# Query and key stacks sent group by group through a ring of five, the experts' bias as one product over 24 rows, and a moved first half-stack, in a three-layer decoder kernel

## The chip, the cores and the metric

The kernel runs on one core of one Trainium2 chip. The metric is the device time in microseconds (us) of one execution, lower being better. A second, profiled execution gives the trace that is read here.

## The reference, cut to what matters

The input is x, 8 batches of 512 tokens by 256 features, and a context of the same shape. Three layers follow each other, each ending in x = layernorm(x + layer(x)):

```
layer 1: q,k,v = x@Wq+bq, x@Wk+bk, x@Wv+bv (128 wide); state = 0.99*state + 0.01*v k^T
         out_t = state_{t-1} q_t ; y = out@Wo + bo
layer 2: 16 heads of 16, q from x, k and v from ctx: softmax(q k^T / 4) v, then @w_o + b_o
layer 3: attn = softmax(q k^T / 4) v with 16 heads, q,k,v from x@W_qkv+b
         gate = softmax(x@W_gate+b); combine = the two largest gates of 8, others 0
         moe = sum_e combine_e * (x@W_e + b_e)          (b_e: the experts' bias, 8x256)
         layer = attn + moe
```

## The kernel before, in words

There are two attentions for each of the 8 batches, so 16 phases in the order C0, C1, S0, C2, S1, ..., S7 (C is the cross attention of layer 2, S the self attention of layer 3). A phase has 4 groups of 4 heads, and a group takes 4 slots, one for each block of 128 keys. A slot has two halves; "slot 82.1" below is the second half of slot 82. In each half TensorE (PE in the profile) computes in this order: two score products into the PSUM tile `sc` (`scores`, two heads, once ScalarE has taken the exponentials of the half before), two products into `mx` for the row maxima of the group that is 6 slots ahead (`max_tiles`), and in the first half of a slot the eight products of probabilities and values into `op` (`values`). VectorE (DVE) reduces each `mx` tile to a maximum; ScalarE (ACT) takes the exponential of `sc`. `max_tiles` waits until the tile two back has been reduced, as there are three `mx` banks.

Everything else is cut into units (a projection, four transposes, an expert product `moe0` to `moe15`, ...), and tables such as `LIN`, `MID_LONG` (batches 1 to 6), `MID_SHORT` (batches 0 and 7) and `MOE_LONG` place each in a slot and half relative to the phase of its batch. `plan_units` makes one list out of it, sorted by half and, within a half, by the loops' order (shift, moe, middle units, first-layer units, heads). TensorE runs the units of both halves of a slot in the second half, after `sc` and `mx`. Units use two PSUM banks of the tile `ms` in turn, so a unit waits until the unit two places ahead of it in the list has been taken out (`unit`: `wait_unit_out(pe, *ORDER[u - 2])`). For the split units (`kc`, `qc`, `k3c`, `q3c`, which make the rows of the half-stacks) taken out means that ScalarE wrote the high part (`high`, L698) and after it VectorE the low part (`low`, L838). For `be0`, `be1` it means ScalarE's copy into `moe`.

The two parts of q and k are then stacked on partitions: 16 high rows, 16 rows of the other part and 16 again for each of the two sides, 48 rows in all, in the tiles `qs` and `ks`. This is done by transfers within SBUF, issued by the SP queue in program order (`stack`, L399): six for a half-stack of two groups, 128 KB each, into a ring of three half-stacks. The row maxima of a group go through a transposition (`shift` unit, L552), a copy to `shift_r` (L892) and two more SP transfers (`shift`, L410) into `qs`; the first score of a group waits for them. In the table a group g has its `shift` unit in slot 4g-2 and its first score in slot 4g.

The gate's choice of experts runs on VectorE in `choose` and `choose_end` (L1011 to L1042), whose last result is `comb`. The unit `combT` transposes `comb` (L594), and `be0`, `be1` multiply it with the 8x256 bias in plain fp32, which the profile shows as two passes for each product (four instructions in a unit).

Of the kernel before, what the change touches and what calls it, by code (L numbers as in the profile page):

```python
# [25 lines left out]
PAIRS = H // SIDES  # L26
HALF = PAIRS // DC
RING = 3
# [22 lines left out]
LIN_SECOND = {"q1": (-13, 1), "k1": (-6, 1), "v1": (-14, 0), "s0": (-5, 1), "s1": (-4, 1), "s23": (-3, 1),  # L51
# [182 lines left out]
STAGED = ("we", "wqkv3")  # L234
# [8 lines left out]
def decoder(nc, x, xT, ctxT, w, out):  # L243
    with ExitStack() as ctx:
# [21 lines left out]
        combT = o1T[0:E, :]  # L266
# [6 lines left out]
        qs = sb("qs", [P, RING, HALF, T])  # L273
        ks = sb("ks", [P, RING, HALF, T])
# [21 lines left out]
        above = sb("above", [P, TB, E, E])  # L296
        tied = sb("tied", [P, TB, E, E])
        rank = sb("rank", [P, TB, E])
        comb = sb("comb", [P, TB, E])
        moe = sb("moe", [P, 2, 512])  # L300
        we_part = (sb("we_hi", [P, DC, E * D]), sb("we_lo", [P, DC, E * D]))
# [12 lines left out]
        w_first, w_in, w_late, we_in = sem("w_first"), sem("w_in"), sem("w_late"), sem("we_in")  # L314
        scaled, we_cut, w3_in, w3_cut, fills = sem("scaled"), sem("we_cut"), sem("w3_in"), sem("w3_cut"), sem("fills")
        x_in, xT_in, ctx_in, y_out = sem("x_in"), sem("xT_in"), sem("ctx_in"), sem("y_out")
        stack_in = {"k": sem("stack_k_in"), "q": sem("stack_q_in")}
# [16 lines left out]
        G_STEPS = 12  # L334
# [30 lines left out]
        def stack_of(g):  # L365

            return 2 * (g // G) + g % G // 2

        @block.sync
        def _(sp):  # L370
# [16 lines left out]
            def stack(name, e):  # L387

                dst, which = (ks, K_PART) if name == "k" else (qs, Q_PART)
                sp.wait_ge(part_low[name], e + 1)  # L390
                if e == 0:
                    sp.wait_ge(fills, 5)
                if e >= RING:
                    sp.wait_ge(score, 2 * 8 * (e - RING + 1))
                    sp.wait_ge(max_t, 32 * (e - RING + 1))
                for side in range(SIDES if (name, e) != ("q", 0) else 1):
                    for r in range(TERMS):
                        at = 64 * side + HD * r
                        sp.dma_start(dst[at:at + HD, e % RING, :, :],  # L399
                                     part[name][64 * side:64 * side + 64, which[r], :]).then_inc(stack_in[name], 16)  # L400

            def shift(g):

                sp.wait_ge(shift_out, g + 1)
                wide = HG // SIDES
                first = wide * (g % 2)
                for side in range(SIDES):
                    at = 64 * side + ROWS
                    rows = SHIFT * wide * TB
                    sp.dma_start(qs[at:at + SHIFT, stack_of(g) % RING, first:first + wide, :]  # L410
                                 .rearrange("a h (n t) -> a (h n) t", n=TB),
                                 shift_r[rows * side:rows * side + rows, g % 2, :]).then_inc(shift_in[g % 2], 16)
# [21 lines left out]
            for c in range(DC):  # L434
                sp.dma_start(we_stage[c], w["we"][:, c, :]).then_inc(we_in, 16)
            for t in range(FIRST_HALF, LAST_HALF + 1):
# [12 lines left out]
        def _(pe):  # L449
# [55 lines left out]
            def unit(task, n):  # L505
# [85 lines left out]
                elif task == "combT":  # L591
                    pe.wait_ge(g_step, G_STEPS * (n + 1))
                    for t in range(TB):
                        last = nc.tensor.transpose(bank[0:E, t * P:t * P + P], comb[:, t, :], ident[:])  # L594
                elif task in ("be0", "be1"):
                    wait_unit_out(pe, "combT", n)
                    for j in range(2):
                        t = 2 * int(task[2]) + j
                        last = mm(bank[:, j * D:j * D + D], combT[:, t * P:t * P + P], W["be"][:], True, True)
# [13 lines left out]
            def max_tiles(i):  # L613

                g, pair, t, _ = head_tile(i)
                e = stack_of(g)
                if i % 32 == 0:
                    for name in "kq":
                        pe.wait_ge(stack_in[name], 16 * TERMS * SIDES * (e + 1))
                if i >= 2:  # L620
                    pe.wait_ge(max_out, i - 1)
                for side in range(SIDES):
                    at = 64 * side
                    mm(mx[:, (i + side) % 3, :], qs[at:at + ROWS, e % RING, 2 * (g % 2) + pair, t * P:t * P + P].bitcast(F32R),
                       ks[at:at + ROWS, e % RING, 2 * (g % 2) + pair, :].bitcast(F32R), True, True).then_inc(max_t, 1)

            def scores(s, h):

                g, kb = s // TB, s % TB
                e = stack_of(g)  # L630
# [4 lines left out]
                for side in range(SIDES):  # L635
                    at = 64 * side
                    last = mm(sc[:, side, :],
                              ks[at:at + ROWS + SHIFT, e % RING, 2 * (g % 2) + h, kb * P:kb * P + P].bitcast(F32R),
                              qs[at:at + ROWS + SHIFT, e % RING, 2 * (g % 2) + h, :].bitcast(F32R), True, True)
# [54 lines left out]
        def _(act):  # L694
# [5 lines left out]
            def high(task, n):  # L700
# [4 lines left out]
                if e >= 1:  # L705
                    act.wait_ge(stack_in[name], 16 * TERMS * SIDES * e)
# [3 lines left out]
            def take_out(task, n):  # L710
# [23 lines left out]
                elif task == "combT":  # L734
                    wait_unit(act, task, n)
                    copy(combT, bank[0:E, :]).then_inc(done, 1)
# [6 lines left out]
                elif task.startswith("moe"):  # L743
# [3 lines left out]
                    act.wait_ge(g_step, G_STEPS * (n + 1))  # L747
# [41 lines left out]
            for t in range(FIRST_HALF, LAST_HALF + 1):  # L789
# [28 lines left out]
                if t == lin_at("qc0", 0) + 1:  # L818
                    act.wait_ge(part_low["q"], 1)
                    for i in range(TERMS):  # L820
                        act.dma_start(qs[64 + HD * i:64 + HD * i + HD, 0, :, :],
                                      part["q"][64:128, Q_PART[i], :]).then_inc(stack_in["q"], 16)
# [8 lines left out]
        def _(dve):  # L831
# [172 lines left out]
            def choose(n):  # L1004
# [17 lines left out]
                nc.vector.tensor_tensor(above[:], theirs, mine, ALU.is_gt).then_inc(g_step, 1)  # L1022
                nc.vector.tensor_tensor(tied[:], theirs, mine, ALU.is_equal).then_inc(g_step, 1)

            def choose_end(n):

                def g_wait(k):
# [4 lines left out]
                nc.vector.tensor_tensor(tied[:].rearrange("p n e m -> p n (e m)"),  # L1032
                                        tied[:].rearrange("p n e m -> p n (e m)"), earlier, ALU.mult) \
                    .then_inc(g_step, 1)
                g_wait(9)
                nc.vector.tensor_tensor(above[:], above[:], tied[:], ALU.add).then_inc(g_step, 1)
                g_wait(10)
                nc.vector.tensor_reduce(rank[:], above[:], AX_X, ALU.add).then_inc(g_step, 1)
# [3 lines left out]
                nc.vector.scalar_tensor_tensor(out=comb[:], in0=rank[:], scalar=2.0, in1=g_p[:],  # L1042
                                               op0=ALU.is_lt, op1=ALU.mult).then_inc(g_step, 1)

            nc.vector.memset(oT[:], 0.0).then_inc(zeros, 1)
            dve.wait_ge(w_in, 16 * len(EARLY))
            for t in range(FIRST_HALF, LAST_HALF + 1):
# [4 lines left out]
                if t == 2 * G:  # L1052
                    dve.wait_ge(w3_cut, 4)
                units = UNITS.get(t - 1, [])
# [111 lines left out]
def head_rows(a):  # L1166

    return a.reshape(DC, H // DC // SIDES, SIDES, HD, -1).transpose(0, 2, 3, 1, 4).reshape(D, -1)
# [45 lines left out]
```

## Time and profile before

| | |
|---|---|
| runs | 1264.37, 1267.0, 1269.11 us; median 1267.0 us |
| profiled execution | 1266.94 us, span 1265.0 us |
| busy share of the span | TensorE 96%, VectorE 71%, ScalarE 61%, GpSimd 29% |
| granted clock of TensorE, mean | 0.996 of full speed |

The busy share of TensorE counts instructions whose ends are modelled, so 96% does not say that its array is at its peak. Rows name a start in us from the span's start, a duration, an engine (PEld is TensorE's weight load, SPq the SP queue issuing transfers), a line of the kernel, and the tiles written and read.

### The profile page before, as it was taken

Reading aid. Unit: us, or ns where it says so; the run is one execution under the profiler, and the core shown is the slowest. Engines: PE = TensorE matmul, PEld = TensorE weight load, DVE = VectorE, ACT = ScalarE, POOL = GpSimd, SP = SyncE. Lnnn points to the kernel's source line nnn. Section 1 sums busy time; section 2 is a strip of 40 time slices with the busy share of each in tenths; the row PEclk is TensorE's granted clock in tenths of the full one; section 3 lists DMA queues with packets and bytes.
Section 4 is the critical chain, followed back from the end, with each engine's and each line's share of the span. In section 5 each row is a group of like instructions: output and inputs, shape, how many; then the busy total and the mean of one; then the engine's idle time right before and its main releaser. Section 6 shows DMA issues by size and latency. Waiting matters only on the chain.

```text
span 1265.0 us, 19962 instructions
## 1 busy us (share of the span) xinstructions
PE 1220.8 (96%) x6936; PEld 601.8 (48%) x6936; DVE 902.8 (71%) x1836; ACT 771.1 (61%) x1072; POOL 366.0 (29%) x471
## 2 busy tenths in 40 slices
PE   8889999999999999999999999999999999999998
PEld 4433444544555445454554545454454534544443
DVE  2577886677777787777776777767877787667772
ACT  2255556666675765756657665666657576655664
POOL 6410103211621134320522206221153204430261
PEclk9899999999999999999999999999999999999999
DMA  7825034313233342233333143332223333303300
GB/s 254 135 43 94 18 52 68 51 29 76 50 69 52 51 85 42 51 45 70 68 67 61 20 74 68 68 52 45 51 42 51 52 52 52 68 2 52 52 19 18
DMA packets 50243, 74.92 MB, mean 59 GB/s; under 512 B 8536, under 2 KB 20320, under 8 KB 49888
## 3 DMA queue, kind: packets, MB, share of 16 engines
q1 hardware_dynamic: 48896, 72.72, 32.8%
q10 hardware_dynamic: 1248, 0.92, 0.4%
q8 instruction: 57, 0.93, 0.4%
q14 instruction: 42, 0.34, 0.1%
HBM read 18.04 MB, written 4.19 MB: 18 GB/s over the span
## 4 chain that ended last, share of the span: by engine, by line
PE 83%; DVE 7%; ACT 5%; issue 3%; DMA 1%; ACTq 0%; POOL 0%; SPq 0%; DVEq 0%
PE ms L451 38%; PE op L451 17%; PE sc L451 15%; PE mx L451 9%; DVE maxes L928 3%; ACT probs L759 2%; PE ms L557 2%; PE ms L502 1%; ACT moe L752 1%; PE ms L552 1%; DMA qs<-q_parts 1%; DMA w_ident<-in_ident 1%; DVE k_parts L838 0%; ACT x L777 0%; DVE heads L901 0%
## 5 line engine op out<-in xcount | busy, mean ns | idle before, releaser
L928 DVE TENSOR_REDUCE maxes<-mx 128x1 f32<-128x512 f32 x1024 | 657.4, 683 | 215.3 <-PE mx L451 213.4
L759 ACT ACTIVATE probs<-sc 128x1024 f32<-128x1024 f32 x512 | 524.3, 1024 | 373.8 <-PE sc L451 368.3
L1131 POOL TENSOR_TENSOR x<-x,moe 128x256 f32<-128x256 f32 x256 | 187.4, 732 | 687.0 <-ACT moe L752 666.5
L451 PE MATMUL op<-probs,v 128*32 128x512 f32 x2048 | 273.6, 606 | 2.9 <-ACT oT L697 2.5
L451 PE MATMUL sc<-qs,ks 50*128 50x512 f32 x1024 | 256.7, 497 | 11.9 <-ACT probs L759 10.3
L451 PEld LDWEIGHTS sc<-qs,ks 50*128 50x128 f32 x1024 | 95.4, 183 | 308.4 <-ACT probs L759 231.5
L451 PE MATMUL mx<-ks,qs 48*128 48x512 f32 x1024 | 209.0, 402 | 10.9 <-DVE maxes L928 8.9
L752 ACT ACTIVATE moe<-ms,comb 128x256 f32<-128x256 f32 x256 | 106.8, 472 | 22.1 <-PE ms L451 22.1
L451 PEld LDWEIGHTS mx<-ks,qs 48*128 48x128 f32 x1024 | 97.7, 187 | 20.8 <-DVE maxes L928 14.7
L451 PE MATMUL ms<-we_hi,x2T_hi 128*128 128x512 f32 x256 | 93.7, 447 | 2.5 <-DVE shift_r L892 1.3
L451 PEld LDWEIGHTS op<-probs,v 128*32 128x32 f32 x2048 | 40.5, 108 | 96.4 <-issue 95.0
L451 PE MATMUL ms<-we_hi,x2T_lo 128*128 128x512 f32 x256 | 80.5, 396 | 0.0
L451 PE MATMUL ms<-we_lo,x2T_hi 128*128 128x512 f32 x256 | 80.3, 394 | 0.0
L451 PEld LDWEIGHTS ms<-we_hi,x2T_hi 128*128 128x128 f32 x256 | 39.1, 188 | 35.4 <-issue 18.8
L451 PEld LDWEIGHTS ms<-we_lo,x2T_hi 128*128 128x128 f32 x256 | 48.0, 188 | 11.8
L451 PEld LDWEIGHTS ms<-we_hi,x2T_lo 128*128 128x128 f32 x256 | 48.0, 188 | 11.7
L838 DVE SCALAR_TENSOR_TENSOR k_parts<-ms,w_bk,k_parts 128x512 fp32r<-128x512 f32 x32 | 24.0, 751 | 33.7 <-ACT k_parts L698 33.3
L1093 POOL TENSOR_SCALAR var<-mv 128x4 f32<-128x4 f32 x24 | 5.5, 230 | 125.8 <-DVE mv L959 110.7
L557 PE MATMUL ms<-w_ident,oT 128*128 128x128 f32 x256 | 39.9, 279 | 1.8 <-DVE shift_r L892 1.0
L698 ACT ACTIVATE k_parts<-ms,w_bk 128x512 fp32r<-128x512 f32 x32 | 22.0, 687 | 32.1 <-PE ms L451 27.3
L844 DVE TENSOR_TENSOR v<-ms,w_bv 128x512 f32<-128x512 f32 x32 | 22.1, 690 | 27.2 <-PE ms L451 27.2
L557 PEld LDWEIGHTS ms<-w_ident,oT 128*128 128x128 f32 x256 | 29.5, 140 | 20.3 <-DVE shift_r L892 14.5
(131 smaller groups left out, 1264.8 us busy)
## 6 DMA issues: line engine op xcount, KB each, us to landing
ks<-k_parts SPq DMA_DIRECT2D x192, 128.0 KB, 4.2
qs<-q_parts SPq DMA_DIRECT2D x189, 128.0 KB, 4.6
xT_s<-in_xT SPq DMA_DIRECT2D x8, 512.0 KB, 3.8
x_s<-in_x SPq DMA_DIRECT2D x8, 512.0 KB, 4.0
ctxT_s<-in_ctxT SPq DMA_DIRECT2D x8, 512.0 KB, 4.2
out<-x SPq DMA_DIRECT2D x7, 512.0 KB, 2.9
qs<-shift_r SPq DMA_DIRECT2D x128, 8.0 KB
probs<-in_we SPq DMA_DIRECT2D x1, 1024.0 KB, 7.1
```

The lines of the kernel that those rows point to most:

```text
L451: return nc.tensor.matmul(dst, lhsT, rhs, start=first, stop=last, skip_group_check=True)
L502: last = nc.tensor.transpose(bank[:, t * P:(t + 1) * P], src[:, t, c * P:(c + 1) * P], ident[:])
L552: last = nc.tensor.transpose(bank[0:SHIFT * HG * TB, 0:P], shift_n[:, n % 2].rearrange("p s a m -> p (s a m)"), ident[:])
L557: last = nc.tensor.transpose(bank[:, t * P:t * P + P], oT[:, t * P:t * P + P], ident[:])
L698: return nc.scalar.activation(dst, src, ACT.Identity, bias=bias, scale=1.0)
L752: nc.scalar.activation(moe[:, k % 2, j * D:j * D + D], bank[:, j * D:j * D + D], ACT.Copy, scale=comb[:, t, e:e + 1]).then_inc(moe_out, 1)
L759: nc.scalar.activation(probs[:, (2 * s + h) % 3, :, :], sc[:], ACT.Exp).then_inc(exp_out, 1)
L838: nc.vector.scalar_tensor_tensor(out=part[name][:, 1, :].bitcast(F32R), in0=unit_bank((task, n)), scalar=bias[:, c:c + 1], in1=part[name][ ...
L844: return nc.vector.tensor_tensor(dst[:, 2 * h:2 * h + 2, 0:H * VW].rearrange("p n (h d) -> p n h d", h=H)[:, :, :, 0:HD], unit_bank((task, ...
L928: nc.vector.tensor_reduce(maxes[:, g % 2, at:at + 1], mx[:, i % 3, :], AX_X, ALU.max).then_inc(max_out, 1)
L1093: nc.gpsimd.tensor_scalar(var[:, k, :], mv[:, k, :, 1], EPS, None, ALU.add).then_inc(step, 1)
L1131: nc.gpsimd.tensor_tensor(x2[:, n % 2, t, :], x2[:, n % 2, t, :], moe[:, k % 2, j * D:j * D + D], ALU.add).then_inc(acc, 1)
```

## The change

Stacks. A transfer now carries one group (32 source rows, 64 KB), so a half-stack takes twelve issues on SP instead of six. The ring has five groups. The second group's issues stand in the SP list right behind the first's while the ring is new, and otherwise one slot after the group five back has ended. Each of q and k has two semaphores, one for even and one for odd groups. `high` waits for both groups of the half-stack before.

Bias. `choose_end` makes three copies of `comb` as high, low and high parts (`comb3`, three more VectorE instructions for each batch), `combT` transposes 24 rows, and `be0`, `be1` are single-pass fp32r products over 24 rows. The bias parts are made once by three VectorE instructions at slot 4. The comparisons of `choose` now use the `moe` buffer. `combT` of batches 1 to 6 moves from slot (33, 1) to (34, 0), where the unit `k3c0` already stands.

Start. `qc1` of batch 0 moves from (-7, 1) to (-6, 1), `k1`, `s0`, `s1` of batch 1 about a slot later, `kc0` of batch 1 from (2, 1) to (1, 1).

```diff
-RING = 3
+WIDE = HG // SIDES
+RING = 5
...
-             ... "qc1": (-7, 1),
+             ... "qc1": (-6, 1),
-LIN_SECOND = {"q1": (-13, 1), "k1": (-6, 1), "v1": (-14, 0), "s0": (-5, 1), "s1": (-4, 1), "s23": (-3, 1),
-              "o1": (-2, 1), "y01": (-1, 1), "y23": (0, 1), "kc0": (2, 1), ...
+LIN_SECOND = {"q1": (-13, 1), "k1": (-5, 1), "v1": (-14, 0), "s0": (-4, 1), "s1": (-3, 0), "s23": (-3, 1),
+              "o1": (-2, 1), "y01": (-1, 1), "y23": (0, 1), "kc0": (1, 1), ...
...
-            "gate": (29, 0), "gateT": (31, 0), "combT": (33, 1), ... "k3c0": (34, 0), ...
+            "gate": (29, 0), "gateT": (31, 0), "combT": (34, 0), ... "k3c0": (34, 0), ...
...
-                    halves["sp"][at(f"{name}{c}", n) + 1].append(("stack_" + kind, 2 * PHASE[layer, n] + c))
+                    t, g = at(f"{name}{c}", n), 4 * PHASE[layer, n] + 2 * c
+                    halves["sp"][t + 1].append(("stack_" + kind, g))
+                    halves["sp"][max(t + 1, 2 * 4 * (g + 1 - RING + 1) + 2) if g >= RING else t + 1].append(("stack_" + kind, g + 1))
...
-                for side in range(SIDES if (name, e) != ("q", 0) else 1):
+                if g >= RING:
+                    sp.wait_ge(score, 2 * TB * (g - RING + 1))
+                    sp.wait_ge(max_t, HG * TB * (g - RING + 1))
+                for side in range(SIDES if (name, g) != ("q", 0) else 1):
                     for r in range(TERMS):
                         at = 64 * side + HD * r
-                        sp.dma_start(dst[at:at + HD, e % RING, :, :],
-                                     part[name][64 * side:64 * side + 64, which[r], :]).then_inc(stack_in[name], 16)
+                        src = 64 * side + first
+                        sp.dma_start(dst[at:at + HD, g % RING, :, :],
+                                     part[name][src:src + 32, which[r], :]).then_inc(stack_in[name][g % 2], 16)
...
-                        last = mm(bank[:, j * D:j * D + D], combT[:, t * P:t * P + P], W["be"][:], True, True)
+                        last = mm(bank[:, j * D:j * D + D], combT[:, t * P:t * P + P].bitcast(F32R), be_part[:].bitcast(F32R),
+                                  True, True)
...
+                g_wait(COMB_STEP)
+                if n >= 1:
+                    wait_unit(dve, "combT", n - 1)
+                nc.vector.tensor_copy(comb3[:, :, 0:E].bitcast(F32R), comb[:]).then_inc(g_step, 1)
+                g_wait(COMB_STEP + 1)
+                nc.vector.tensor_tensor(comb3[:, :, E:2 * E].bitcast(F32R), comb[:], comb3[:, :, 0:E],
+                                        ALU.subtract).then_inc(g_step, 1)
+                nc.vector.tensor_copy(comb3[:, :, 2 * E:3 * E].bitcast(F32R), comb3[:, :, 0:E]).then_inc(g_step, 1)
```

## Rows read from the trace of the kernel before

**Rows 1.** The page: busy time of the engines; shares of the chain that ended last.

```profile
PE 1220.8 (96%) x6936; PEld 601.8 (48%) x6936; DVE 902.8 (71%) x1836; ACT 771.1 (61%) x1072; POOL 366.0 (29%) x471
...
PE 83%; DVE 7%; ACT 5%; issue 3%; DMA 1%; ACTq 0%; POOL 0%; SPq 0%; DVEq 0%
```

**Rows 2.** Timeline of batch 2, slots 81.1 to 82.1: start, us, engine, line, tiles.

```profile
453.90 0.19 DVE L1042 SCALAR_TENSOR_TENSOR comb<-rank,g_p 128x32 f32<-128x32 f32 x1
...
454.23 0.60 PE L594 MATMUL ms<-w_ident,comb 128*8 128x128 f32 x4
...
455.10 0.41 PE L451 MATMUL mx<-ks,qs 48*128 48x512 f32 x2
...
456.43 0.50 PE L451 MATMUL sc<-qs,ks 50*128 50x512 f32 x2
...
457.56 0.74 PE L451 MATMUL ms<-x2T_hi,w_hi 128*128 128x512 f32 x2 [0.16 <-ACT o1T L697]
...
459.06 0.60 PE L557 MATMUL ms<-w_ident,oT 128*128 128x128 f32 x4
459.32 0.69 ACT L698 ACTIVATE k_parts<-ms,w_bk 128x512 fp32r<-128x512 f32 x1 [0.91 <-PE ms L451]
...
460.04 0.75 DVE L838 SCALAR_TENSOR_TENSOR k_parts<-ms,w_bk,k_parts 128x512 fp32r<-128x512 f32 x1 [1.36 <-ACT k_parts L698]
```

**Rows 3.** Timeline around bias units of batch 2, and fp32r products over 256 columns.

```profile
170.88 0.40 PE L451 MATMUL ms<-w_lo,x2T_hi 128*128 128x256 f32 x2
...
467.09 0.75 DVE L838 SCALAR_TENSOR_TENSOR q_parts<-ms,bq3s,q_parts 128x512 fp32r<-128x512 f32 x1
...
467.24 1.13 PE L451 MATMUL ms<-w_be,o1T 8*128 8x256 f32 x4
...
468.30 0.73 PE L451 MATMUL ms<-we_hi,x2T_hi 128*128 128x512 f32 x2
...
474.08 0.79 PE L451 MATMUL ms<-we_hi,x2T_hi 128*128 128x512 f32 x2
```

**Rows 4.** Tile `ks`: duration of one issue in ns, least, median, most.

```profile
L399 SPq DMA_DIRECT2D ks<-k_parts x192: 547/597/1104, 27.4 to 1178.2; - x192
```

**Rows 5.** Timelines: SP's issues and the first score of groups 6, 20, 52, 60.

```profile
160.46 3.80 SPq L399 DMA_DIRECT2D ks<-k_parts  x6
...
176.49 0.50 PE L451 MATMUL sc<-qs,ks 50*128 50x512 f32 x2
...
432.56 3.75 SPq L399 DMA_DIRECT2D qs<-q_parts  x6
441.77 1.34 SPq L410 DMA_DIRECT2D qs<-shift_r  x2
...
445.78 0.50 PE L451 MATMUL sc<-qs,ks 50*128 50x512 f32 x2
...
1029.83 3.75 SPq L399 DMA_DIRECT2D qs<-q_parts  x6
1037.85 16.30 SPq L410 DMA_DIRECT2D qs<-shift_r  x4
...
1040.60 0.50 PE L451 MATMUL sc<-qs,ks 50*128 50x512 f32 x2 [0.75 <-DMA qs<-shift_r]
...
1179.58 3.75 SPq L399 DMA_DIRECT2D qs<-q_parts  x6
...
1192.48 0.50 PE L451 MATMUL sc<-qs,ks 50*128 50x512 f32 x2
```

**Rows 6.** Timeline of batch 0, first half of slot 24.

```profile
177.73 0.49 PE L451 MATMUL mx<-ks,qs 48*128 48x512 f32 x2 [0.74 <-DVE maxes L928]
```

**Rows 7.** The start: the chain in order of time.

```profile
34.70 8.27 DMA qs<-q_parts
...
45.15 3.71 PE ms L451 x4
```

**Rows 8.** Windows: busy us (instructions) by engine, granted clock, DMA share, GB/s.

```profile
43.00:46.00 3.00, 2.14 (x5) 1.00 (x6) 2.39 (x4) 1.06 (x2) 3.00 (x1) 0.64 1.07 129
```

More of the change, by code:

```diff
@@ L233 @@
 EARLY = ("wv1", "bv1", "decay", "wo1", "bo1", "ident")
-STAGED = ("we", "wqkv3")
+STAGED = ("we", "wqkv3", "be")
 def head_tile(i):
@@ L265, in decoder @@
         o1T = sb("o1T", [P, T])
-        combT = o1T[0:E, :]
+        combT = sb("combT", [TERMS * E, T])[:]
         gateT = sb("gateT", [P, P])[:]
@@ L300, in decoder @@
         moe = sb("moe", [P, 2, 512])
+        above, tied = (moe[:, 0, k * TB * E * E:(k + 1) * TB * E * E].rearrange("p (n e f) -> p n e f", n=TB, e=E) for k in range(2))
+        comb3 = sb("comb3", [P, TB, TERMS * E])
+        be_part = sb("be_part", [TERMS * E, D])
+        be_stage = moe[0:TERMS * E, 1, 0:D]
         we_part = (sb("we_hi", [P, DC, E * D]), sb("we_lo", [P, DC, E * D]))
@@ L314, in decoder @@
         w_first, w_in, w_late, we_in = sem("w_first"), sem("w_in"), sem("w_late"), sem("we_in")
+        be_in, be_cut = sem("be_in"), sem("be_cut")
         scaled, we_cut, w3_in, w3_cut, fills = sem("scaled"), sem("we_cut"), sem("w3_in"), sem("w3_cut"), sem("fills")
         x_in, xT_in, ctx_in, y_out = sem("x_in"), sem("xT_in"), sem("ctx_in"), sem("y_out")
-        stack_in = {"k": sem("stack_k_in"), "q": sem("stack_q_in")}
+        stack_in = {name: [sem(f"stack_{name}_in{n}") for n in range(2)] for name in "kq"}
         shift_in = [sem(f"shift_in{n}") for n in range(2)]
@@ L593, in unit @@
                     for t in range(TB):
-                        last = nc.tensor.transpose(bank[0:E, t * P:t * P + P], comb[:, t, :], ident[:])
+                        last = nc.tensor.transpose(bank[0:TERMS * E, t * P:t * P + P], comb3[:, t, :], ident[:])
                 elif task in ("be0", "be1"):
                     wait_unit_out(pe, "combT", n)
+                    if n == 0:
+                        pe.wait_ge(be_cut, 3)
                     for j in range(2):
                         t = 2 * int(task[2]) + j
-                        last = mm(bank[:, j * D:j * D + D], combT[:, t * P:t * P + P], W["be"][:], True, True)
+                        last = mm(bank[:, j * D:j * D + D], combT[:, t * P:t * P + P].bitcast(F32R), be_part[:].bitcast(F32R),
+                                  True, True)
                 else:
@@ L623, in max_tiles @@
                     at = 64 * side
-                    mm(mx[:, (i + side) % 3, :], qs[at:at + ROWS, e % RING, 2 * (g % 2) + pair, t * P:t * P + P].bitcast(F32R),
-                       ks[at:at + ROWS, e % RING, 2 * (g % 2) + pair, :].bitcast(F32R), True, True).then_inc(max_t, 1)
+                    mm(mx[:, (i + side) % 3, :], qs[at:at + ROWS, g % RING, pair, t * P:t * P + P].bitcast(F32R),
+                       ks[at:at + ROWS, g % RING, pair, :].bitcast(F32R), True, True).then_inc(max_t, 1)
             def scores(s, h):
                 g, kb = s // TB, s % TB
-                e = stack_of(g)
                 if 2 * s + h >= 1:
@@ L705, in high @@
                 if e >= 1:
-                    act.wait_ge(stack_in[name], 16 * TERMS * SIDES * e)
+                    for signal in stack_in[name]:
+                        act.wait_ge(signal, 16 * TERMS * SIDES * e)
                 wait_unit(act, task, n)
@@ L735, in take_out @@
                     wait_unit(act, task, n)
-                    copy(combT, bank[0:E, :]).then_inc(done, 1)
+                    copy(combT.bitcast(F32R), bank[0:TERMS * E, :]).then_inc(done, 1)
                 elif task in ("be0", "be1"):
@@ L746, in take_out @@
                     wait_unit(act, task, n)
-                    act.wait_ge(g_step, G_STEPS * (n + 1))
+                    act.wait_ge(g_step, G_STEPS * n + COMB_STEP)
+                    if n == 0:
+                        act.wait_ge(be_cut, 3)
                     if k >= 2:
@@ L821, in _ @@
                         act.dma_start(qs[64 + HD * i:64 + HD * i + HD, 0, :, :],
-                                      part["q"][64:128, Q_PART[i], :]).then_inc(stack_in["q"], 16)
+                                      part["q"][64:96, Q_PART[i], :]).then_inc(stack_in["q"][0], 16)
                 if t == lin_at("kc1", 0) + 1:
@@ L1021, in choose @@
                 theirs = g_p[:].rearrange("p n (o e) -> p n o e", o=1).broadcast_to([P, TB, E, E])
-                nc.vector.tensor_tensor(above[:], theirs, mine, ALU.is_gt).then_inc(g_step, 1)
-                nc.vector.tensor_tensor(tied[:], theirs, mine, ALU.is_equal).then_inc(g_step, 1)
+                if n >= 1:
+                    dve.wait_ge(acc, 2 * MOE_ENTRIES * n)
+                else:
+                    dve.wait_ge(w3_cut, 4)
+                nc.vector.tensor_tensor(above, theirs, mine, ALU.is_gt).then_inc(g_step, 1)
+                nc.vector.tensor_tensor(tied, theirs, mine, ALU.is_equal).then_inc(g_step, 1)
             def choose_end(n):
@@ L1031, in choose_end @@
                 earlier = W["earlier"][:].rearrange("p (o m) -> p o m", o=1).broadcast_to([P, TB, E * E])
-                nc.vector.tensor_tensor(tied[:].rearrange("p n e m -> p n (e m)"),
-                                        tied[:].rearrange("p n e m -> p n (e m)"), earlier, ALU.mult) \
+                nc.vector.tensor_tensor(tied.rearrange("p n e m -> p n (e m)"),
+                                        tied.rearrange("p n e m -> p n (e m)"), earlier, ALU.mult) \
                     .then_inc(g_step, 1)
                 g_wait(9)
-                nc.vector.tensor_tensor(above[:], above[:], tied[:], ALU.add).then_inc(g_step, 1)
+                nc.vector.tensor_tensor(above, above, tied, ALU.add).then_inc(g_step, 1)
                 g_wait(10)
-                nc.vector.tensor_reduce(rank[:], above[:], AX_X, ALU.add).then_inc(g_step, 1)
+                nc.vector.tensor_reduce(rank[:], above, AX_X, ALU.add).then_inc(g_step, 1)
                 g_wait(11)
@@ L1053, in _ @@
                     dve.wait_ge(w3_cut, 4)
+                    dve.wait_ge(be_in, 16)
+                    nc.vector.tensor_copy(be_part[:].bitcast(F32R), be_stage).then_inc(be_cut, 1)
+                    dve.wait_ge(be_cut, 1)
+                    nc.vector.tensor_scalar(be_stage, be_stage, W["side"][:, 0:1], None, ALU.mult).then_inc(be_cut, 1)
+                    dve.wait_ge(be_cut, 2)
+                    nc.vector.scalar_tensor_tensor(out=be_part[:].bitcast(F32R), in0=be_part[:], scalar=W["side"][:, 1:2],
+                                                   in1=be_stage, op0=ALU.mult, op1=ALU.add).then_inc(be_cut, 1)
                 units = UNITS.get(t - 1, [])
@@ L1198 @@
         "we": by_chunk(arr(ffn + "W_experts").transpose(1, 0, 2).reshape(D, E * D)),
-        "be": arr(ffn + "b_experts"),
+        "be": np.tile(arr(ffn + "b_experts"), (TERMS, 1)),
+        "side": np.repeat(np.array([[0, 1], [0, 1], [1, -1]], np.float32), E, 0),
         "ident": np.eye(P, dtype=np.float32),
```

41 lines of the change are left out of this document (16 added, 25 removed), and 6 rows, old and new, of tables (LIN_FIRST, LIN_SECOND, MID_LONG).

## The prediction

> **What bounds the kernel now.** I read the page first. TensorE is busy for 96% of the span and makes 83% of the chain that ended last [rows 1], so time is won only where TensorE does less, and lost wherever it is made to wait. Which of its waits are full is then a matter of single halves of a slot, so I read the timeline half by half. A half without units lasts about as long as one loop through ScalarE (score, exponential, next score), so a short unit that stands alone in a half is almost free, and one beside others costs its full time. Then I read what stands behind TensorE: the wait for the unit two places ahead, VectorE's reductions, and the SP queue, whose issues are not counted as busy anywhere and must be read in its own timeline.
>
> **Bias products.** A bias unit of four fp32 instructions holds TensorE from 467.24 to 468.30, 1.06 us [rows 3]. Two fp32r products over 256 columns are busy for 0.40 us in all and follow each other closer than that; the lower bound of their cost is nothing, and I take 0.3 us, so 0.76 us would be saved. But the next unit also waits for the one two places ahead. In `be0`'s half that is `q3c0`, whose low part ends at 467.84 [rows 3], so the expert product can start at 467.88 and not before: 468.30 - 467.88 = 0.42 us saved. In `be1`'s half of batches 1 to 5 the units are `be1`, `s0`, `moe3`, and `moe3`, which starts at 474.08 [rows 3], waits for ScalarE's copy of `be1`, which ScalarE begins only after that half's exponential; I take 0.38 us of the 0.76, as for `be0` about half. Batch 6 has no `s0` and saves 0.42 + 0.76. In batch 0 I count 0.3 for `be0` and nothing for `be1` (the unit behind it waits for `shift`'s copy anyway), in batch 7 nothing, since what it saves is waited away at group 60, below. Sum: 5 x 0.80 + 1.18 + 0.3 = 5.5 us saved. Bounds: 4.0, and 15 x 0.76 = 11.4 if no second wait existed.
>
> **Three more instructions in choose_end.** One on 128x32 costs 0.19 us [rows 2], and with the wait for the one before about 0.22: 0.6 us on VectorE. In batches 0 and 7 `choose_end` already makes TensorE wait 0.74 us for a maximum [rows 6], so 0.6 more would be lost twice; the late shifts below cover both, and if that cover is gone they cost 1.2 us.
>
> **combT beside k3c0.** The list of slot 82 becomes shift, k3c0, combT, heads, where it was shift, k3c0, heads with combT a slot earlier. Two places ahead of heads now stands k3c0, not shift. So heads must wait for ScalarE's high and VectorE's low part of k3c0. Step by step for batch 2, by its rows [rows 2]:
> Slot 81.1 loses combT (454.23, 0.60 us) and its wait for `comb`, so its successor's score comes earlier, but the maxima decide. VectorE ends choose_end 0.6 later than 454.09, at 454.70, so its next maximum (0.6 us) frees a bank at about 455.28, and `mx` of slot 82.0 starts at 455.30, not 455.10. The score of 82.1 starts at 456.62 instead of 456.43: +0.19. In 82.1, k3c0 starts 0.16 sooner within its half, at 457.36. ScalarE's high part starts 1.76 after k3c0 (459.32 - 457.56), and the low part ends 1.47 after that start (460.79 - 459.32), so at 460.59. Heads starts at 460.62 instead of 459.06: +1.56 us. Four things are in it: the wait (about 1.1), combT's own 0.4, which lies inside the wait's cover, and the 0.19. Queued behind heads on TensorE is everything, so all of it is lost, in each of batches 1 to 6: 6 x 1.56 = 9.4 us. Bounds: nothing, if the drain of k3c0 could be earlier, and 12.
>
> **The stacks.** The bytes are the same, and the maxima get their rows in time. What grows is SP's issuing. One issue takes 0.597 us [rows 4], six take 3.75 to 3.80 [rows 5], 0.63 each with the gap. Does half the size cost half? The nearest row says no: the two transfers of `shift_r`, of 8 KB each, take 1.34 us for two [rows 5]. I take 0.63 for each of twelve; the lower bound is half of it, 0.31.
> SP works in order, and `shift` stands behind the stacks. Before a cross phase the list is now: the six of `q` for group 4p+2, then twelve for group 4p+3, then `shift` of group 4p. For group 20: 432.56 + 18 x 0.63 = 443.90, where shift was issued at 441.77. From a shift's first issue to the score that it releases takes 1040.60 - 1037.85 = 2.75 us [rows 5] (that score shows its wait for the transfer). So the score of group 20 starts at 446.65 instead of 445.78: +0.87. Groups 12, 28, 36 and 44 repeat it: 5 x 0.87 = 4.4. The slots before group 52 are short: 1029.83 + 18 x 0.63 = 1041.17, + 2.75 = 1043.92 against 1040.60: +3.3. In batch 0 k and q of groups 8 and 9 stand together, 24 issues: 160.46 + 15.12 = 175.58, + 2.75 = 178.33 against 176.49: 1.84, less the 0.74 of [rows 6] that it covers: +1.1. Batch 7 repeats it at group 58, +1.2. Group 60: 1179.58 + 11.34 + 2.75 = 1193.67 against 1192.48: +1.2. Sum 11.2 us. The bounds: nothing with issues under 0.5 us, and about 15 if nothing covers anything.
> The Trainium skill has a sentence that speaks for the other end: in DMA: Bandwidth & Descriptors, section Issuing engines are not separate DMA queues, the sequencer's time to start a DMA is called usually small relative to the DMA. By it the stacks would cost nothing here and the sum would end near 1268; this trace, at 0.6 us an issue, does not make it small.
>
> **The start.** The first maxima wait for the last of q's transfers, which lands at 34.70 + 8.27 = 42.97 [rows 7]. Transfers move some 130 GB/s there [rows 8], and before the first maxima 1.18 MB are needed instead of 1.57 MB, 3.0 us less; k's second group sits in front of q's first in SP's queue, which is in that figure. `qc1`, four instructions of `k1`'s shape, then comes in beside the maxima, 1.9 us at full clock. The granted clock is 0.64 over that window [rows 8], part of it at the lower of its two levels (1.2 of 2.4 GHz) right after TensorE's wait for the transfer. If it stays at the upper level, `k1`'s 3.71 us [rows 7] become 1.9, which pays for `qc1`. I take -3.0 for all of it; bounds -1.1 (the clock falls anyway) and -4.
> Moving `kc0` of batch 1 to slot 1 puts its six k issues in front of `shift` of group 1, which I find some 2 us late, as much as the move itself wins: 0, bounds -2 and +1. The three instructions that cut the bias at slot 4 (1.3 us of VectorE) lie under that same wait; without it +0.5. The comparisons' wait for the experts' sums is satisfied by the tables, 7 slots early.
>
> **Sum.** The profiled execution took 1266.94 us, practically the median of 1267.0: 1266.9 - 5.5 + 9.4 + 11.2 - 3.0 = **1279 us**.
>
> **Rivals.**
> (B) Issues cost by size, 0.31 us. This ends on the other side, not slower. For it speaks that a smaller copy has fewer packets; against it the 8 KB shift. It decides from about 0.5 us an issue down: 1279 - 11.2 - (0 to 2) + 1.2 (choose_end uncovered) = 1267 to 1269, no change.
> (C) heads does not wait: if its bank is free earlier, 1.1 x 6 = 6.6 go, 1272.4. Against it stand the 0.91 and 1.36 us that ScalarE and VectorE idle before k3c0's parts [rows 2]: they cannot come sooner than TensorE allows.
> (D) The new waits of 2 to 3 us pull TensorE's clock down, as at 43 us. Each drop costs about 2 us: with two or three 1284.
> (E) B and C together, and the whole gain at the start: 1260.
>
> **How the numbers follow.** The forecast (A) has 0.50, B 0.18, C 0.14, D 0.10, E 0.08. A alone spans 1273 to 1284. From B's low edge to above A and D the range is 1264 to 1285, which leaves out E and a little of D. A change under 0.5% (6.3 us) can't be told from none by this measurement. Slower by more: A, D and a small part of C, 0.64. Within: B and most of C, 0.28. Faster: E, 0.08.
>
> **What would show it.** Right: SP's stack issues at about 0.6 us each, twelve in a row; scores of groups 6, 12, 20, 52, 58, 60 with a wait for the transfer of shift_r; six waits of about 1.1 us of the heads transposes (L557) for k_parts on VectorE; bias products of two instructions; first maxima at about 40 us. Wrong: 64 KB issues at 0.3 us, no wait before heads, or first maxima still at 43 us.

## The result, and the profile after

The changed kernel takes 1304.5 us (1299.8 to 1305.7, 4 runs) against 1267.8 us of the kernel before on the same chip: a ratio of 1.0287, 95% interval 1.0253 to 1.0321. Forecast were 1279 us and a range up to 1285. The direction was right; the size was three times the forecast. One execution in the whole study (1283.3 us, of the kernel with all repairs) was in a second, slower state with a mean clock of 0.944 and is left out of the times.

The page of the changed kernel: busy time, the shares of the chain that ended last, the group of scores with the idle time before it, and the transfers (number, size, us from issue to landing).

```profile
PE 1224.3 (94%) x6904; PEld 601.6 (46%) x6904; DVE 912.4 (70%) x1863; ACT 770.8 (59%) x1072; POOL 364.6 (28%) x471
...
PE 71%; SPq 10%; DVE 8%; ACT 4%; issue 4%; DMA 3%; POOL 0%; ACTq 0%; DVEq 0%
...
L452 PE MATMUL sc<-qs,ks 50*128 50x512 f32 x1024 | 259.3, 502 | 36.8 <-DMA qs<-shift_r 25.3
...
ks<-k_parts SPq DMA_DIRECT2D x384, 64.0 KB, 2.2
qs<-q_parts SPq DMA_DIRECT2D x381, 64.0 KB, 2.2
```

Beside [rows 1] TensorE is busy no less, but its share of the chain fell from 83 to 71%, and SPq, which had none, has 10%: a queue that the busy list doesn't even name now sets the end for 130 us. The view of waits (who waited for whom: us in total, times, longest) says on what:

```profile
PE sc L452 <- DMA qs<-shift_r: 25.3, 13, 5.2
...
PEld ms L558 <- DVE k_parts L843: 8.3, 6, 1.4
...
PE ms L558 <- DVE k_parts L843: 6.6, 6, 1.1
```

In the kernel before the first of these stood at 0.7 us, once, and the other two not at all. The tile `ks`, as [rows 4], shows twice the issues at the same duration each, half the bytes notwithstanding, and one as long as 1.7 us:

```profile
L401 SPq DMA_DIRECT2D ks<-k_parts x384: 558/592/1692, 27.5 to 1223.2; - x192
```

The largest loss is at the shift of group 1, 5.1 us in slot 3.1; the timeline of SP, then TensorE's:

```profile
77.25 7.95 SPq L401 DMA_DIRECT2D ks<-k_parts  x12
85.24 1.32 SPq L410 DMA_DIRECT2D qs<-shift_r  x2
```

```profile
81.41 3.05 PE L452 MATMUL ms<-w_wv,ctxT_s 128*128 128x256 f32 x8
87.98 0.80 PE L452 MATMUL sc<-qs,ks 50*128 50x512 f32 x2 [3.52 <-DMA qs<-shift_r]
```

VectorE had `shift_r` ready at 78.60; SP issued it at 85.24. What came with an idle TensorE is in the windows (length, then busy us of PE, PEld, DVE, ACT, POOL, the granted clock, DMA share, GB/s):

```profile
76.00:80.00 4.00, 2.54 (x21) 0.80 (x17) 3.32 (x7) 4.00 (x7) 0.00 (x0) 1.00 0.16 37
80.00:84.00 4.00, 3.84 (x15) 2.67 (x12) 2.72 (x6) 1.23 (x2) 0.00 (x0) 0.57 0.45 104
84.00:88.00 4.00, 0.48 (x5) 0.11 (x3) 0.69 (x1) 0.00 (x0) 0.00 (x0) 0.87 0.36 82
88.00:92.00 4.00, 4.00 (x16) 1.18 (x16) 1.29 (x2) 1.19 (x2) 1.22 (x2) 0.50 0.34 115
92.00:96.00 4.00, 4.00 (x22) 2.91 (x24) 1.92 (x3) 2.14 (x4) 1.56 (x3) 0.77 0.00 0
...
1066.00:1070.00 4.00, 0.04 (x1) 0.00 (x0) 1.75 (x6) 0.62 (x1) 0.00 (x0) 1.00 0.42 98
1070.00:1074.00 4.00, 2.73 (x12) 0.73 (x12) 1.29 (x2) 1.14 (x2) 0.00 (x0) 0.50 0.01 2
```

The clock fell at 80.2 us for 3.4 us, before this wait and behind an idle time of 1.46 us, and again at 87.0 for 6.8 us, behind it. From 84 to 88 us TensorE did next to nothing, and from 88 to 92 it ran at 0.50, the lower of its two levels (1.2 of 2.4 GHz), so that a pair of scores took 0.80 us, not 0.50. At 1066, before group 52, the same again.

**Where the 38.5 us of span went**, read half by half, from one pair of scores to the next, in both traces (the halves that hold it in brackets). Waits for `shift_r`: 25.0 us (3.1 +5.1, 23.1 +2.8, 207.1 +4.5, 231.1 and 232.0 +2.1, 239.1 +1.5, and 0.3 to 2.1 in front of groups 12, 16, 20, 24, 28, 36, 40 and 44). Halves behind such waits that run at the lower level: 9.8 us (seven of 1.3 to 1.6). combT's new place: 10.3. The bias products: -5.9. The rest, start and singles: -0.7.

The second of these terms can be checked without any trace, since each execution comes with its mean granted clock, and the kernel before alone gave these medians in the runs of this study:

| mean clock | 1.000 | 0.999 | 0.995 | 0.993 | 0.985 |
|---|---|---|---|---|---|
| kernel before, us | 1263.0 | 1264.5 | 1268.7 | 1269.9 | 1277.5 |

At 0.984 the changed kernel took 1305.4, 28 us above the kernel before at 0.985; at 0.991 it took 1299.8, again 28 to 29 above 1271.3 at 0.992 (one execution). The step of 0.001 between the clocks of each pair is worth 0.9 us by the table. So of the 36.7 us between the medians 27 to 28 are work and waits, and 9 to 10 are the clock. Below, "at the same clock" means a pair with equal clocks.

### The profile page after: what moved, and what is told of

It is laid out like the page before. It is cut to its first block, busy times and chain, and to the rows that moved or that the text cites. A ratio compares the mean times of both kernels' runs of the same rounds, so it can differ in the third digit from the quotient of the medians.

```text
span 1303.6 us, 20431 instructions
## 1 busy us (share of the span) xinstructions
PE 1224.3 (94%) x6904; PEld 601.6 (46%) x6904; DVE 912.4 (70%) x1863; ACT 770.8 (59%) x1072; POOL 364.6 (28%) x471
## 4 chain that ended last, share of the span: by engine, by line
PE 71%; SPq 10%; DVE 8%; ACT 4%; issue 4%; DMA 3%; POOL 0%; ACTq 0%; DVEq 0%
PE ms L452 32%; PE op L452 14%; PE sc L452 13%; SPq L401 9%; PE mx L452 8%; DVE maxes L933 3%; DMA qs<-shift_r 2%; PE ms L558 2%; ACT probs L764 1%; PE ms L503 1%; DVE k_parts L843 1%; DVE q_parts L843 1%; ACT q_parts L700 1%; ACT k_parts L700 1%; PE ms L553 1%
## 5 line engine op out<-in xcount | busy, mean ns | idle before, releaser
L558 PE MATMUL ms<-w_ident,oT 128*128 128x128 f32 x256 | 40.3, 280 | 9.0 <-DVE k_parts L843 6.6
L558 PEld LDWEIGHTS ms<-w_ident,oT 128*128 128x128 f32 x256 | 29.0, 141 | 28.1 <-DVE shift_r L897 14.9
```

What stands on the lines that cost most here:

```text
L558: last = nc.tensor.transpose(bank[:, t * P:t * P + P], oT[:, t * P:t * P + P], ident[:])
```

## The experiments

Times are medians; the kernel before stood at 1267 to 1269 in every comparison.

**The stacks alone.** The changed kernel's `stack`, `shift`, ring and semaphores with everything else as before.

> The stacks alone (64 KB transfers, ring of five groups, the second group's issues where the change puts them), with the bias products, combT and the tables of the kernel before. Theory 1 (SP's issues stand in front of shift): the time is lost here. Scores of groups 6, 12, 20, 28, 36, 44, 52, 58, 60 wait for the transfer of shift_r, about 20 us in all; group 1 does not, since kc0 of batch 1 stands at slot 2 and its issues come behind that shift (in the changed kernel that group alone lost 5 to 7 us); the waits of 2 us and more pull the granted clock down, some 5 to 8 us; the first maxima come 3 us sooner. Together 1285 to 1292 us. Rival (the clock falls for another reason, and the stacks cost only the waits beyond the prediction's 11 us): about 1278. Rival (the stacks are harmless, combT's place or the start makes the loss): 1265 to 1269.

Measured: 1294.2 us, ratio 1.0216 (1.0171 to 1.0261), 18.5 to 19 us above before at the same clock. Eleven groups wait:

```profile
PE sc L448 <- DMA qs<-shift_r: 21.8, 11, 4.9
```

The stacks carry most of the loss, 2 us beyond the expectation's end. Group 1 has no such wait here, as expected. The first score comes 2.1 us sooner.

**The stacks alone, second group behind the shift.**

```diff
- halves["sp"][max(t + 1, 2 * 4 * (g + 1 - RING + 1) + 2) if g >= RING else t + 1].append(("stack_" + kind, g + 1))
+ halves["sp"][max(t + 1, 2 * 4 * (g + 1 - RING + 1) + 6) if g + 1 >= RING else t + 1].append(("stack_" + kind, g + 1))
```

> The stacks alone (the run at 1294 us), but the second group's issues behind the next shift, none in front of it. As many issues and bytes, ring and sizes as in that run. Theory 1 (all of the stacks' 25 us were issues in front of shift, with the falls of the clock that they brought): no wait for shift_r, one or two falls of the clock, the start 1 to 2 us sooner: span 1261 to 1265, 1263 to 1269 in the median, the same as before. Rival (765 issues instead of 381, or transfers of half the size, cost by themselves): 1275 or more.

Measured: 1268.6 us, ratio 1.0012 (0.9995 to 1.0030), at the same clock 0.3 to 0.6 us above before, and 1.5 us at 0.993. SP's timeline at group 20, where the shift now goes first:

```profile
442.61 1.31 SPq L407 DMA_DIRECT2D qs<-shift_r  x2
444.03 0.38 SPq L382 DMA_DIRECT2D ctxT_s<-in_ctxT  x1
444.51 4.07 SPq L398 DMA_DIRECT2D ks<-k_parts  x6
448.69 3.73 SPq L398 DMA_DIRECT2D qs<-q_parts  x6
```

The same 765 issues of 64 KB, their size and the ring of five now cost no more than that: 25 us hang on one line, on the number that places the second group and the condition in front of it. Which share the condition has was not tried by itself.

**Twice the issues in the old places.** The kernel before with each 128 KB transfer issued as two of 64 KB, side by side.

```diff
-                        sp.dma_start(dst[at:at + HD, e % RING, :, :],
-                                     part[name][64 * side:64 * side + 64, which[r], :]).then_inc(stack_in[name], 16)
+                        for q in range(2):
+                            src = 64 * side + 32 * q
+                            sp.dma_start(dst[at:at + HD, e % RING, 2 * q:2 * q + 2, :],
+                                         part[name][src:src + 32, which[r], :]).then_inc(stack_in[name], 16)
```

> The kernel before, ring of three half-stacks, tables and places as they were, but each 128 KB transfer issued as two of 64 KB, one for each group, side by side: as many issues as in the changed kernel. Theory 1 (what costs is how many issues stand between the list's start and shift, and the change put the second group's twelve there): only where a run of 12 or 24 reaches a shift is it late: group 6 and 58 by 1 to 3 us, group 1 not, the others not at all (twelve issues in 7.6 us end before shift's place): 1269 to 1274. Rival (twice as many issues cost time wherever they stand, by SP or by the DMA engines): 1285 or more.

Measured: 1278.9 us, ratio 1.0082 (1.0056 to 1.0108); 6 us above before at a clock of 0.995. Five groups wait, where thirteen did in the change:

```profile
PE sc L453 <- DMA qs<-shift_r: 8.9, 5, 2.6
```

They are 6 and 58, as expected, 52 and 60, which I had not named, and 3 with 0.2 us. Group 20 is free: its twelve issues end at 441.4 and its shift goes at 442.1. The time lies 5 us above the expectation, by those two groups and the clock.

**The changed kernel, second group behind the shift.** The same edit as above in the whole change.

> The changed kernel with the second group's issues one place later, behind the shift that stood after them (+ 6 halves in place of + 2), and the condition taken for the second group, so that group 5's issues no longer stand in front of shift of group 1. As many issues and bytes. Theory 1: the 25 us of waits for shift_r are gone but for a few us, and so are the clock's falls that they made (10 to 20 us of the 41 at the lower level); what remains is heads' wait (+10) and the bias' gain (-6): 1268 to 1274. Rival (the number of issues or the transfers themselves slow the kernel wherever they stand): above 1290. Rival (the clock falls for another reason): 1278 to 1284 with the waits gone.

Measured: 1279.2 us, ratio 1.0081 (1.0048 to 1.0114). No wait for `shift_r` is left in the trace. It gives back 25 us of the 37, though 5 us less than I expected: heads' waits cost more than my 10 us (next), and 20.5 us are still spent at the lower level, twice as much as before, though no wait for `shift_r` is there to explain it.

**The bias alone**, with combT at (34, 0); `comb3` lies in the tile of `gateT`, since with three half-stacks there is no room for it.

> The bias alone (24 rows, fp32r products, three more VectorE instructions, combT of batches 1 to 6 at slot (34, 0)), with the stacks and tables of before; comb3 lies in the tile of gateT for want of room. Theory 1: six waits of 1.1 to 1.4 us before the heads transposes for k_parts (+10), the products save 5.9: +4, about 1271.5. Rival (the waits before heads are absorbed by waits that follow them): 1261 to 1263. Rival (VectorE's three instructions cost as much again in every batch): 1276.

Measured: 1276.8 us, ratio 1.0068 (1.0045 to 1.0092). The time is that of the third case, though mostly by another mechanism. Half by half each of batches 1 to 6 loses 2.27 us from slot 81.1 to 82.1 (-0.64, +1.03, +1.88 in batch 2; of these only the first two, +0.4, are VectorE's) and wins 0.87 at be0 and be1: 13.6 - 5.9 in all. In the changed kernel the same term is 10.3, since in batches 4 to 6 the loss is 1.3, 1.3 and 0.7; what covers it there I did not trace.

**combT back at (33, 1) in the changed kernel.**

```diff
-            ... "combT": (34, 0), ...
+            ... "combT": (33, 1), ...
```

> The changed kernel with combT of batches 1 to 6 back at slot (33, 1), a slot half before k3c0. Theory 1 (heads waits for k_parts because k3c0 stands two places ahead of it): the six waits at L558 for k_parts are gone, slot 82.1 loses 1.9 us and 82.0 1.0, slot 81.1 gets back 0.65 and some 0.5 more, since combT now waits for comb3: 1.7 each, 10 in all, 1294 us. Rival (the three instructions of comb3 hold up VectorE and the maxima, and it is they that cost): 1302 to 1305, slots 81 and 82 together no shorter.

Measured: 1295.2 us, ratio 1.0223 (1.0177 to 1.0269); at the same clock (0.984) 9.4 us below the changed kernel. The six waits at L558 are gone, slot 82.1 has lost 1.92 us and 82.0 1.03, and 81.1 has gained 1.19. Theory 1 holds; the half microsecond left in 81.1 is combT's wait for `comb3`.

**combT ahead of k3c0.** Three more kernels tried combT's place. The first two put it ahead of k3c0 in the list: in the bias alone, and in the changed kernel with the second group behind the shift.

```diff
-        units.sort(key=lambda unit: not soon(*unit))
+        units.sort(key=lambda unit: (not soon(*unit), unit[0] not in ("shift", "combT")))
```

> The bias alone (as in the run of the bias alone, 1276.8 us), combT in slot (34, 0) but in the list ahead of k3c0, so that combT, not k3c0, stands two places ahead of heads. Theory 1: heads waits for a short ScalarE copy that is done by then; each batch gets back about 2 of its 2.27 us: 12 us, 1264 to 1266, faster than before by the bias products alone. Rival (comb3 on VectorE or the crowded half costs it): 1272 or more.

> The changed kernel with both repairs: the second group's issues behind the next shift, and combT ahead of k3c0 in its half. Theory 1: 1279.2 less 12 = 1266 to 1268, the same as before within the measurement; what is left above the bias' gain is the clock's four falls (20.5 us at the lower level against 10.2) and the start tables. Rival (the two repairs overlap, since the waits of heads cover something): 1272 to 1276.

Measured: 1276.8 us (ratio 1.0062, 1.0029 to 1.0096) and 1277.1 us (1.0073, 1.0044 to 1.0102): nearly nothing won, 0.25 us in most batches. I had freed heads and caught k3c0, which now has `shift` two places ahead:

```profile
459.58 0.27 DVE L901 COPY shift_r<-ms 32x128 f32<-32x128 f32 x1
...
459.90 0.74 PE L455 MATMUL ms<-x2T_hi,w_hi 128*128 128x512 f32 x2 [0.91 <-DVE shift_r L901]
```

The wait had not gone, it had changed its unit; slot 82.0 kept its +1.03. There it is VectorE: with `comb3` it ends choose_end later, and `mx` of that half waits 0.76 us for it.

**comb3 later, combT at (35, 0).** The three instructions stand in a task of their own one and a half slots behind choose_end, and combT beside moe1 and q3c0.

```diff
-            ... "combT": (34, 0), ... "choose_end": (33, 0)}
+            ... "combT": (35, 0), ... "choose_end": (33, 0), "parts": (34, 1)}
```

> The bias alone, with the stacks and tables of before; the three instructions that make comb3 stand one and a half slots behind choose_end in VectorE's list, and combT of batches 1 to 6 at slot (35, 0), between moe1 and q3c0, away from heads. Theory 1: neither VectorE's maxima nor heads wait any longer, combT costs its 0.4 us in slot 83.1 instead of 0.65 in 81.1, and the products save 0.87 for a batch: 6 us less than before, 1260 to 1263. Rival (what the products save is waited away whatever stands around): 1267 to 1269. Rival (three more VectorE instructions cost the path 0.4 us or more wherever they stand): 1264 to 1266.

Measured: 1269.3 us, ratio 1.0025 (0.9998 to 1.0053), where 6 us less than before were expected. The deferral halves slot 82.0's loss (+0.50), and together with combT's absence (-0.64 in 81.1, -0.27 in 82.1) slots 81 and 82 are 0.4 us shorter than before. But slot 83.1 loses 1.41, not 0.4.

**The changed kernel with all repairs**: both of the above edits' effects (shift first; comb3 later, combT at (35, 0)) and the start tables of before.

> The changed kernel with all four repairs: the second group's issues behind the next shift, comb3 later, combT at (35, 0), the start tables of before. Theory 1: no wait for shift_r, no wait of heads; the bias' 6 us and 2 us of the start are kept: 1257 to 1262, faster than both. Rival (falls of the clock take back what is gained): 1265 to 1270. Rival (twice the issues cost by themselves): 1270 or more.

Measured: 1265.6 us, ratio 0.9992 (0.9969 to 1.0014): by the two ratios 37 us below the change, and no faster than before (at the same clock 0.5 to 1.1 us above it). The number lies where the rival of the falling clock put it, but its cause is not there: the profiled execution has one fall of 3.4 us before its end, where the kernel before has three times that. TensorE's timeline in slot 83.1 shows the same rule a third time:

```profile
460.96 0.60 PE L595 MATMUL ms<-w_ident,comb 128*24 128x128 f32 x4
...
462.05 0.73 PE L452 MATMUL ms<-x2T_hi,w_hi 128*128 128x512 f32 x2 [0.49 <-ACT moe L757]
```

Two places ahead of q3c0 now stands moe1, which ScalarE is still taking out; in the kernel before it was heads.

**combT ahead of moe1**, by the sorting line above in this kernel: k3c0 two places ahead of combT, heads ahead of moe1, combT ahead of q3c0.

> The run with all four repairs again, but combT of batches 1 to 6 ahead of moe1 in slot 83.1, not behind it. There q3c0 stood two places behind moe1 and waited 0.5 to 0.8 us for ScalarE's copy of it, so that combT cost 1.4 us in that half instead of its 0.4. Theory 1 (the wait for the unit two places ahead decides, not the 0.4 us of combT's own): 1.0 us less in each of six batches, a span of 1257 to 1258 against 1263.4, 1259 to 1263 in the median of the runs. Rival (combT costs what stands around it, wherever it is put): unchanged at 1267.

Measured: 1265.6 us, ratio 0.9988 (0.9971 to 1.0004), the profiled span 1260.8; at the same clock 1.3 to 1.8 us below before. The wait of q3c0 is gone, moe1's is 0.18:

```profile
457.62 0.61 PE L595 MATMUL ms<-w_ident,comb 128*24 128x128 f32 x4
...
458.42 0.74 PE L452 MATMUL ms<-we_hi,x2T_hi 128*128 128x512 f32 x2 [0.18 <-DVE heads L906]
...
459.93 0.62 PE L452 MATMUL ms<-x2T_hi,w_hi 128*128 128x512 f32 x2
```

Slot 83.1 still loses 1.00, so the repair gave 0.4 us a batch where I expected 1.0: neither theory had the size. Each of batches 1 to 5 is now 0.3 us shorter than before (0.27 to 0.35), of the 0.88 that the products save.

**The start tables.** Alone on the kernel before, and taken out of the change.

> The tables of the start alone (qc1 of batch 0 and k1, s0, s1, kc0 of batch 1 moved), with everything else of before. Theory 1: the first maxima wait as long as before for their 1.57 MB, kc0's six k issues stand in front of the shift of group 1 and make it some 2 to 3 us late, qc1 beside the maxima costs up to 1.9 us: 1267 to 1270. Rival (the tables win the 1.4 us that slots 1 to 3 showed and qc1 is free): 1265.

> The changed kernel with the two tables of the start as before (qc1 of batch 0 beside nothing, kc0 of batch 1 at slot 2). Theory 1: the six k issues of group 5 no longer stand in front of shift of group 1, whose wait of 5.2 us goes, and with it the clock's fall at 80 and 87 us: slots 0 to 16 last 66 to 67 us instead of 74.5, 1295 to 1297 us in all. Rival (the new tables are what gains the 3 us at the first maxima, so without them the start is later): slot 0 at 68 us or later, 1300 or more.

Measured: 1275.2 us, ratio 1.0056 (1.0032 to 1.0080), and 1299.0 us, 5 and 2 us above the expectations. Alone the tables lose 4.2 us at the same clock: the six k issues make the shift of group 1 2.5 us late,

```profile
78.57 3.80 SPq L399 DMA_DIRECT2D ks<-k_parts  x6
82.42 1.35 SPq L410 DMA_DIRECT2D qs<-shift_r  x2
```

and slot 3.1 is 3.6 us longer, followed by the lower level. SP's lateness is not all of it. TensorE's timeline, the window 80 to 84 us (columns as above) and the k transfers of this stretch (the last number is us from issue to landing):

```profile
87.72 0.79 PE L451 MATMUL sc<-qs,ks 50*128 50x512 f32 x2 [3.48 <-DMA qs<-shift_r]
```

```profile
80.00:84.00 4.00, 3.85 (x24) 1.90 (x20) 2.58 (x4) 2.55 (x4) 0.00 (x0) 1.00 0.99 148
```

```profile
ks<-k_parts SPq DMA_DIRECT2D x6, 128.0 KB, 4.4
```

From the shift's issue to its score it takes 5.30 us here (87.72 - 82.42), and 2.74 in the change (87.98 - 85.24). The six k transfers of 128 KB are issued 0.64 us apart but land 1.0 us apart, the last at 86.99, and keep the DMA engines busy (0.99); behind them the shift's own 8 KB land late. Of the wait of 3.48 us about 2.6 are this, by the difference of the two times. The twelve transfers of 64 KB in the change land as they are issued, 0.63 us apart, at a DMA share of 0.45. So bytes set the wait behind 128 KB transfers, and issues behind 64 KB ones.

Taken out of the change, the tables leave slots 0 to 15 at 66.7 us instead of 74.5, as expected, and the first score comes at 65.1, not later than in the change (66.6). Of these 9.4 us only 5.6 reach the end: slots 24 to 30 lose 2.4 of them again, where the clock falls at 201.6 us for 6.8 us, and later stretches the rest.

## Why the forecast was too low

**The shifts (forecast +11.2, measured +25.0): the step that failed.** Its mechanism held: 0.6 us an issue whatever its size, in SP's order, waits at all six groups named. Its terms did not.
- Group 1 was costed at nothing, "its six k issues in front of shift of group 1, some 2 us late, as much as the move itself wins". There were twelve: the condition `g >= RING` looks at the half-stack's first group, 4, so group 5's issues stand at once behind them. +5.1 us, the largest single loss, and I had the line in front of me. Six issues instead of twelve make the shift 2.5 us late, as the tables alone show; with 64 KB transfers that would have been a wait of about 0.9 us, an estimate from that run's times with 2.74 us to the score. The 3.6 us that the tables alone lose there hold the transfers of 128 KB still under way as well.
- Groups 16 and 24, left out of the sum, lost 0.92 and 0.95 like groups 12, 20 and 28 (0.95 to 1.04, forecast 0.87).
- Groups 36, 44 and 52 met an issue of 1.4 to 1.8 us instead of 0.6: 2.1, 1.8 and 4.5 us for 0.9, 0.9 and 3.3. Such issues were there before too, up to 1.1 us in the row of `ks` [rows 4] and up to 1.9 us in that of `qs`; I summed medians. Group 6 cost 2.8 for 1.1: its 24 issues took 16.1 us, not 15.1, and slot 24.0, whose 0.74 us of wait I subtracted as covered, was as long as before. Groups 58 and 60 cost 2.1 and 1.5 for 1.2 each.

**The clock (a rival at 0.10, "each drop costs about 2 us: with two or three 1284"): it came, and more often.** It is not an alternative to the waits but for the most part their consequence: with the waits taken out, the stacks alone went from 37.5 us at the lower level to 13.7, and the changed kernel from 41.0 to 20.5, where the kernel before has 10.2. It cost 9 to 10 us by the comparison at the same clock, 9.8 by halves, some 1.1 us for each 3.4 us more at the lower level, and not 2. In the sum the clock stood at nothing: the forecast held a late score of 3.3 us and did not price what falls behind it. This is the second term that failed.

**combT beside k3c0 (forecast +9.4, measured +10.3).** Right in its cause; heads' own wait is 1.10 us as foreseen:

```profile
470.82 0.50 PE L452 MATMUL mx<-ks,qs 48*128 48x512 f32 x2 [0.24 <-DVE maxes L933]
...
472.88 0.61 PE L595 MATMUL ms<-w_ident,comb 128*24 128x128 f32 x4
474.59 0.66 PE L558 MATMUL ms<-w_ident,oT 128*128 128x128 f32 x4 [1.10 <-DVE k_parts L843]
```

What the working lacked is the second loss, VectorE's three instructions in front of the maximum of slot 82.0. I counted 0.19 for it; slots 81.1 and 82.0 together lost 0.38, and 82.1 lost 1.9 instead of 1.37. Uncovered, in the bias alone, the sum is 13.6. In batches 1 to 3 of the change the forecast's 1.56 was 0.7 short, in batches 4 to 6 it was 0.2 to 0.9 too much, so that the sum came out near by luck. The working also has a slip: with the score of 82.1 at 456.62, k3c0 starts at 457.59 and not at 457.36, which makes the loss 1.79 a batch and 10.7 in all by its own steps.

**The bias products (forecast -5.5, measured -5.9).** Right, down to be0's 0.42: halves 84.1 and 85.1 are 0.39 and 0.48 shorter.

**The start (forecast -3.0, measured -0.2 at the first score).** The first maxima start at 40.0 us instead of 43.1, as forecast. The clock then falls at 42.6 and 59.7, and the win is spent before slot 0. Across the kernels with the new stacks the first score came at 63.6 to 66.7 us, by where the clock fell. The 63.6, 3.2 us sooner than before, are those of the changed kernel with combT back, whose profiled execution has no fall before slot 0: the forecast's 3.0 holds on its condition, that the clock stays up, and not otherwise.

**The time of an issue.** The Trainium skill (DMA: Bandwidth & Descriptors, section Issuing engines are not separate DMA queues) calls the sequencer's time to start a DMA usually small relative to the DMA. Here it is 0.59 us against 2.2 to landing for 64 KB (0.60 against 4.2 for 128 KB), and twelve in a row are 7.95 us. Small or not, it mattered only where something urgent stood behind: with the shift in front the same issues cost next to nothing.

## What to carry to other kernels

In any queue that also carries something urgent count issues first and then the bytes still under way: here 64 KB transfers were bound by the issues and 128 KB ones by their landing. For each urgent entry list all that stands ahead of it as the code places it, with conditions evaluated for the very first groups; then put bulk behind the urgent one. When two slots or buffers alternate, moving one unit changes who waits for whom three times over: work out the neighbour two places ahead of every unit in the new list before costing anything. Price a wait of a few microseconds on TensorE with the clock that falls behind it (here seven halves of 1.3 to 1.6 us each).

## What the runs showed beyond the question

- The time of an execution follows its mean granted clock closely: the kernel before goes from 1264.5 us at 0.999 to 1277.5 at 0.985, 13.0 us for 17.7 us of clock (0.014 of 1265). Two kernels are best compared at the same value; the last kernel's gain of 1.5 us shows there, and not in its ratio. By the Trainium skill (TensorE: Matmul & The Clock Gate, section Terms) the penalty is about the time at the lower level times one half. By it the estimate would be the 17.7 us; the 13.0 measured are about a quarter less.
- An issue on SP took 0.59 us in the median for 64 KB as for 128 KB, and single ones up to 1.8 us: 23 of 765 were over 0.7 us, and before 11 of 381, up to 1.9 us.
- With one fall of the clock gone another came elsewhere: with the start tables of before the falls at 80 and 87 us went, and the one at 186.0 us (3.4 us) gave place to 177.7 (3.4) and 201.6 (6.8).
